# Causal attention whose softmax sums are gathered and folded by DMA, a streamed tile attention, and weight loads beside the norms

## The reference, cut to what matters

```python
# tile attention: a softmax of its own over each of 8 tiles of 128 keys
k_t = k.reshape(B, T, TILE, D)
v_t = v.reshape(B, T, TILE, D)
scores = jnp.einsum('bqd,btkd->btqk', q, k_t) * scale
w = jax.nn.softmax(scores, axis=-1)
out = jnp.einsum('btqk,btkd->bqd', w, v_t)
norm = w.sum(axis=-1).sum(axis=1)[..., None]
out = out / (norm + 1e-06)
return out @ Wo.T + bo

# causal attention, 16 heads of 8 features
scores = jnp.einsum('blhd,bmhd->bhlm', q, k) * scale
att = jax.nn.softmax(jnp.where(causal, scores, -jnp.inf), axis=-1)
out = jnp.einsum('bhlm,bmhd->blhd', att, v).reshape(B, L, D)
return out @ w_proj.T
```

## Time and profile before

| | |
|---|---|
| median of 3 runs | 5923.98 us (5920.12 to 5926.69) |
| the profiled execution | 5904.04 us, span 5902.2 us |
| granted TensorE clock, mean | 0.946 of full speed |
| busy: TensorE, VectorE, ScalarE, GpSimd | 84%, 68%, 54%, 30% of the span |
| tile attention | 45.9 to 323.4 us |
| the causal attentions | 460.2 to 1041.7 and 1616.8 to 2198.6 us |
| six local layers and the end | from some 2199 us on |

### The profile page before, as it was taken

How to read it: one execution, slowest core, us unless ns; L and a number is a source line. 1 busy time by engine, 2 the same in 40 slices (tenths; PEclk the granted TensorE clock), 3 DMA queues, 4 the chain that set the end, 5 groups by cost and what they waited for, 6 DMA issues and landing times. The chain is left out here.

```text
span 5902.2 us, 168251 instructions
## 1 busy us (share of the span) xinstructions
PE 4957.4 (84%) x74434; PEld 2867.4 (49%) x74640; DVE 3991.8 (68%) x4814; ACT 3191.4 (54%) x3632; POOL 1770.6 (30%) x1242
## 2 busy tenths in 40 slices
PE   6757887788688868998899889988998799979997
PEld 3423332333233325664466546654666366636663
DVE  5767775333477747885788568865887588748884
ACT  2324665222256546774577557754776367637773
POOL 0020000000200005551455235533554155505550
PEclk9988999899789999999999999999999899989998
DMA  0011000000101001111111111110111011101111
GB/s 25 0 53 35 25 24 13 22 0 0 62 18 29 24 30 38 38 38 34 34 37 37 41 27 38 38 45 23 36 37 53 16 38 38 35 30 38 38 38 41
DMA packets 90446, 187.28 MB, mean 32 GB/s; under 512 B 26112, under 2 KB 42368, under 8 KB 87552
## 3 DMA queue, kind: packets, MB, share of 16 engines
q1 hardware_dynamic: 89728, 176.58, 11.3%
HBM read 60.10 MB, written 14.68 MB: 13 GB/s over the span
## 5 line engine op out<-in xcount | busy, mean ns | idle before, releaser
L1413 POOL TENSOR_TENSOR part_of_local<-part_of_local,sine_of_local 128x512 f32<-128x512 f32 x768 | 961.2, 1273 | 1058.7 <-DVE sine_of_local L1350 1058.7
L820 ACT ACTIVATE prob_of_ca<-ps 128x1024 f32<-128x1024 f32 (+3 forms) x768 | 598.8, 814 | 374.9 <-PE ps L667 246.9
L1420 POOL TENSOR_TENSOR part_of_local<-part_of_local,inverse_of_local 128x1024 f32<-128x1024 f32 x384 | 722.5, 1903 | 139.6 <-DVE inverse_of_local L1382 139.6
L1387 DVE TENSOR_REDUCE total_of_local<-prob_of_local 128x16 f32<-128x1024 f32 x192 | 234.3, 1220 | 419.1 <-ACT prob_of_local L1326 419.1
L685 PE MATMUL ps<-keys_of_ca,queries_of_ca 64*128 64x512 bf16 (+3 forms) x1536 | 336.5, 346 | 195.2 <-DVE top_of_ca L858 73.2
L1347 DVE TENSOR_TENSOR part_of_local<-ps,rope 128x1024 f32<-128x1024 f32 x384 | 467.1, 1216 | 41.0 <-ACT square_of_local L1294 41.0
L1350 DVE TENSOR_TENSOR sine_of_local<-ps,rope 128x1024 f32<-128x1024 f32 x384 | 467.0, 1216 | 0.0
L1186 PE MATMUL ps<-qkv,shifted 128*128 128x512 f32 x768 | 392.0, 634 | 88.9 <-POOL values_of_local L1423 78.9
L1196 PE MATMUL ps<-qkv,shifted 128*128 128x512 f32 x768 | 381.0, 619 | 83.4 <-ACT heads_out_of_local L1322 69.3
L1272 PEld LDWEIGHTS ps<-prob_t_of_local,mixed_of_local 64*64 64x64 f32 x12288 | 335.6, 134 | 163.9 <-issue 154.1
L858 DVE TENSOR_REDUCE top_of_ca<-ps 128x2 f32<-128x1024 f32 (+1 forms) x320 | 357.1, 1116 | 70.1 <-PE ps L667 44.9
(11 more groups left out here) (206 smaller groups left out, 10122.5 us busy)
## 6 DMA issues: line engine op xcount, KB each, us to landing
mixed_of_local<-values_of_local SPq DMA_DIRECT2D x636, 128.0 KB
mixed_of_local<-values_of_local SPq DMA_DIRECT2D x264, 64.0 KB
queries_of_ca<-q_parts SPq DMA_DIRECT2D x384, 32.0 KB
keys_of_ca<-k_parts SPq DMA_DIRECT2D x384, 32.0 KB
qkv<-in_qkv SPq DMA_DIRECT2D x7, 1536.0 KB, 6.4
rope<-in_rope SPq DMA_DIRECT2D x7, 1024.0 KB, 9.0
q_parts<-parts_of_ci SPq DMA_DIRECT2D x16, 384.0 KB, 2.5
k_parts<-parts_of_ci SPq DMA_DIRECT2D x16, 384.0 KB, 2.5
```

The source lines that it names most:

```text
L820: nc.scalar.activation(prob[:, i % 2, 2 * two:2 * two + 2, j:], ps[:, 2 * two:2 * two + 2, j:], ACT.Exp, scale=scale).then_inc(raised, 1)
L1413: nc.gpsimd.tensor_tensor(out, out, sine[:, side, :, (1 - to) * half:(2 - to) * half], ALU.add).then_inc(rotated, 1)
L1420: nc.gpsimd.tensor_tensor(part[:, t % 2, side], part[:, t % 2, side], by, ALU.mult).then_inc(scaled, 1)
```

## The change

**Loads.** The first stage loads x in 8 chunks and only three constants; the other constants and the tile attention's weights are fetched by SyncE during `ln0`. The three later load stages of this part go; their DMAs are issued in `ln1`, `ln2` and `ln3`. In `ln1` and `ln2` ScalarE waits for them before it applies the norm's weights.

**Tile attention.** The loop over batches becomes one stage with a stream of 32 tiles. Projections and mixes of neighbouring batches are tasks, one after the score of most tiles, in PSUM bank 7. VectorE takes the maximum and scales it by −scale; ScalarE raises each of the 8 groups of 128 columns straight from PSUM with that as its bias, so the subtraction goes; VectorE makes sum and ratios; GpSimd multiplies the tile by them.

**Causal attention.** SyncE collects each group's sums by 8 DMAs: 8 rows a head into one full tile of 128 rows (`collected`), and the row of totals into DRAM. After the fourth group `fold` fetches the totals as 128x128, VectorE takes one reciprocal, SyncE writes it to DRAM and reads it back as a factor with 8 equal rows a head. GpSimd multiplies in two halves; a mix is one matmul. `collect` stands after `place` in SyncE's program, `fold` after the `collect` of a batch's last group, and both ahead of the next `load_stack`.

```diff
 def layernorm(..., fetches=(), late_weight=False):
...
                 nc.scalar.activation(rstd[:, :], rstd[:, :], ACT.Sqrt).then_inc(rooted, 1)
+                if late_weight:
+                    act.wait_ge(fetched, 16 * len(fetches))
...
 def tile_attention(nc, ps, k, w, xn, out):
-    with nc.Fori(0, B) as b, Stage(nc, "ta") as st:
+    with Stage(nc, "ta") as st:
...
+                for first in FIRST_TASKS:
+                    task(0, *first)
+                for s in range(NT + 3):
+                    if s < NT:
+                        score(s)
+                        if tile_task(s):
+                            task(*tile_task(s))
+                    if 0 <= s - 2 < NT:
+                        turn(s - 2)
+                    if s - 3 >= 0:
+                        gather(s - 3)
+                task(B - 1, "mix", 1)
...
+                def raise_tile(s):
+                    act.wait_ge(shifted, s + 1)
+                    if s >= 3:
+                        act.wait_ge(turned, s - 2)
+                    for j in range(TILES):
+                        last = nc.scalar.activation(prob[:, s % 3, j, :], score_banks(s)[:, j // 4, j % 4 * P:(j % 4 + 1) * P],
+                                                    ACT.Exp, bias=shift[:, s % 2, j:j + 1], scale=scale)
+                    last.then_inc(raised, 1)
...
+                for s in range(NT + 2):
+                    if s - 2 >= 0:
+                        copy_out(s - 2)
+                    if s < NT:
+                        raise_tile(s)
+                        if tile_task(s):
+                            task(*tile_task(s))
...
+                for s in range(NT + 4):
+                    if s < NT:
+                        top_of(s)
+                        if tile_task(s):
+                            task(*tile_task(s))
+                    if 0 <= s - 1 < NT:
+                        ratio_of(s - 1)
+                    if s >= 6 and (s - 6) % 4 == 0:
+                        even((s - 6) // 4)
...
+            @block.gpsimd
+            def _(pool):
+                for s in range(NT):
+                    pool.wait_ge(ratios, s + 1)
+                    nc.gpsimd.tensor_tensor(prob[:, s % 3], prob[:, s % 3], ratio[:, s % 2].unsqueeze(2)
+                                            .to_broadcast([P, TILES, P]), ALU.mult).then_inc(weighed, 1)
...
-FINISH = {(0, 4): ("totals", 0), (0, 5): ("invert", 0), (0, 6): ("invert", 1), (0, 7): ("split", 0), (0, 8): ("split", 1),
-          (1, 4): ("spread", 0), (1, 6): ("spread", 1), (1, 8): ("mix", 0),
-          (2, 4): ("spread", 2), (2, 6): ("spread", 3), (2, 8): ("mix", 1)}
+FINISH = {(0, 5): ("invert", 0), (1, 4): ("mix", 0), (1, 6): ("mix", 1)}
...
+                def collect(G):
+                    b, g = divmod(G, GROUPS)
+                    sp.wait_ge(acc_out, 2 * (G + 1))
+                    if g == 0 and b >= 2:
+                        sp.wait_ge(even, 2 * (b - 1))
+                    for h in range(HG):
+                        of = summed[h * QUAD:h * QUAD + HD + 1, G % 2].rearrange("p a n -> p (a n)")
+                        row = (g * HG + h) * HD
+                        sp.dma_start(collected[row:row + HD, b % 2, :], of[0:HD]).then_inc(collects[G % 2], 16)
+                        sp.dma_start(totals[g * HG + h:g * HG + h + 1, :], of[HD:HD + 1]).then_inc(collects[G % 2], 16)
+
+                def fold(b):
+                    for n in range(2):
+                        sp.wait_ge(collects[n], COLLECTS * 2 * (b + 1))
+                    sp.dma_start(folded[:, :], totals.rearrange("h (a n) -> (h a) n", n=P)).then_inc(totals_in, 16)
+                    sp.wait_ge(inverted, b + 1)
+                    if b:
+                        sp.wait_ge(factor_in, 16 * b)
+                    sp.dma_start(inverses.rearrange("h (a n) -> (h a) n", n=P), inverse[:, :]).then_inc(inverse_out, 16)
+                    sp.wait_ge(inverse_out, 16 * (b + 1))
+                    if b:
+                        sp.wait_ge(even, 2 * b)
+                    sp.dma_start(factor[:, :], inverses.unsqueeze(1).to_broadcast([HEADS, HD, L])).then_inc(factor_in, 16)
+
                 place(0)
-                for G in range(ALL - 1):
+                for G in range(ALL):
                     if G and G + 2 < ALL:
                         sp.wait_ge(scored, 2 * NU * G)
                         load_stack(sp, loaded[(G + 2) % RING_CA], stacks, zeros, q_parts, k_parts, G + 2)
-                    place(G + 1)
+                    if G + 1 < ALL:
+                        place(G + 1)
+                    collect(G)
+                    if G % GROUPS == GROUPS - 1:
+                        fold(G // GROUPS)
...
+                def evens(b):
+                    pool.wait_ge(factor_in, 16 * (b + 1))
+                    if b:
+                        pool.wait_ge(done, 2 * b)
+                    for half in range(2):
+                        nc.gpsimd.tensor_tensor(evened[:, chunk(half)], collected[:, b % 2, chunk(half)],
+                                                factor[:, chunk(half)], ALU.mult).then_inc(even, 1)
+
                 for G in range(ALL):
                     place_values(G)
+                    if G > GROUPS and G % GROUPS == 1:
+                        evens(G // GROUPS - 1)
+                evens(B - 1)
...
                 def mix(b, half):
                     take_lone()
-                    pe.wait_ge(even, 4 * b + 2 * half + 2)
-                    for g in range(GROUPS):
-                        last = nc.tensor.matmul(lone[:, :], proj[:, g, :], evened[:, g, :],
-                                                start=g == 0, stop=g == GROUPS - 1)
-                    last.then_inc(lone_ready, 1)
+                    pe.wait_ge(even, 2 * b + half + 1)
+                    nc.tensor.matmul(lone[:, :], proj[:, :], evened[:, chunk(half)], start=True, stop=True)\
+                        .then_inc(lone_ready, 1)
```

More of the change, by code:

```diff
@@ L212, in tile_attention, with task_bank, score_banks @@
+        FIRST = len(FIRST_TASKS)
+        number, made = {(0, *task): n for n, task in enumerate(FIRST_TASKS)}, FIRST
+        for s in range(NT + TILES):
+            if s < NT and tile_task(s):
+                number[tile_task(s)], made = made, made + 1
+        number[B - 1, "mix", 1] = made
+        def task_bank(n):
+            return ps[:, n if n < FIRST else 7, :]
+        def score_banks(s):
+            return ps[:, s % 2 * 2:s % 2 * 2 + 2, :]
         with nc.Block() as block:
@@ L224, in _, with task @@
[L224 to L228, removed]
+                def task(b, kind, half):
+                    n = number[b, kind, half]
+                    if n >= FIRST:
+                        pe.wait_ge(task_out, n)
+                    to, first = task_bank(n), b * L + half * CH
+                    if kind == "mix":
+                        pe.wait_ge(evened, 2 * b + half + 1)
+                        last = nc.tensor.matmul(to, w["ta_o"][:, :], outT[:, half, :], start=True, stop=True)
+                    elif kind == "v":
+                        for t in range(4):
+                            last = nc.tensor.matmul(to[:, t * P:(t + 1) * P], xn[:, first + t * P:first + (t + 1) * P],
+                                                    w["ta_v"][:, :], start=True, stop=True)
+                    else:
+                        last = nc.tensor.matmul(to, w["ta_" + kind][:, :], xn[:, first:first + CH], start=True, stop=True)
+                    last.then_inc(task_ready, 1)
@@ L261, in _ @@
-                score(0)
-                score(1)
-                for t in range(TILES):
-                    if t + 2 < TILES:
-                        score(t + 2)
-                    if t:
-                        gather(t - 1)
-                    turn(t)
-                    if t == 5:
-                        mix(0)
-                gather(TILES - 1)
-                mix(1)
+                        last = nc.tensor.matmul(ps[:, 6, s % 4 * P:(s % 4 + 1) * P], v[:, s // TILES % 2, j, :],
+                                                probT[:, s % 2, j, :], start=j == 0, stop=j == TILES - 1)
@@ L301, in _, with task @@
-                copy_out(TILES - 1)
-                finish(1)
-                act.wait_ge(written, 2)
+                def task(b, kind, half):
+                    n = number[b, kind, half]
+                    act.wait_ge(task_ready, n + 1)
+                    if kind == "mix":
+                        first = b * L + half * CH
+                        nc.scalar.activation(out[:, first:first + CH], task_bank(n), ACT.Identity,
+                                             bias=w["ta_bo"][:, :]).then_inc(task_out, 1)
+                    elif kind != "v":
+                        to = (qT, kT)[kind == "k"]
+                        nc.scalar.activation(to[:, b % 2, chunk(half)], task_bank(n), ACT.Identity,
```

(4 more changed lines are left out.)

327 lines of the change are left out of this document (114 added, 213 removed).

## The result

The median fell from 5925.33 us (5920.12 to 5931.23, 4 runs) to 5727.31 us (5725.95 to 5731.99, 4 runs): a ratio of 0.9667, 95% interval 0.9650 to 0.9684. The profiled execution took 5725.95, span 5724.2, clock 0.944: 178 us less than the span of before. The forecast was 5742 and the sum 182.

A forecast was written before the change was run, and what follows sets the result against it. It saw no full engine in the tile attention, TensorE and VectorE locked together in the causal attention, and loads standing alone. Gains 29 + 74 + 79 = 182 us took 5904.04 to 5722, plus 19.94 gave 5742, range 5685 to 5812.

The forecast's parts named there:

- last step: Whole kernel: the median lies 19.94 us above the profiled execution, so 5722 becomes 5742.
- loads: Load stages before the norms: loading beside the norms gives back 29 us, between 23 and 34.
- tile attention: Tile attention as one stream: 5.75 us a tile, 203.5 us against 277.5, a gain of 74.
- causal attention, both calls: Causal attention: cheaper batch finishes and a shorter end gain 39.5 us a call, 79 for both.
- the loop of 10.7 for two tiles: Tile attention: a closed loop through TensorE, VectorE and GpSimd takes 10.7 us for two tiles, 5.35 each.
- the plain groups: Causal attention groups without a fold: 0.25 us charged for each of ten stack loads a call.
- The mixes: Causal attention, group after a fold: two mixes, each one matmul and an eviction, cost 1.4 us each, 2.8.
- The term of 8.5: Causal attention, groups 4, 8 and 12: TensorE stands 8.5 us at unit 8 for stacks issued behind the fold.
- The end: Causal attention, last copy to the end of a call: 20.9 us against 29.14, 8.2 less.
- The fold costs nothing: Rival, causal attention: unit 8 isn't late, 2 × 25.5 us more gained, 5691; chance 0.12.
- the queue in every group: Rival, causal attention: SyncE's queue bounds every group, all 26 stack loads land 3 us later, 5815; chance 0.13.
- not streamed: Rival, tile attention: exps or GpSimd's product hold it at 6.6 us a tile, 27 us more, 5769; chance 0.10.

The follow-up runs named there:

- t_more: Changed kernel with an extra GpSimd product of half a tile, into a spare tile, in every tile of the tile attention: 5743.77 us.
- c_mix: Changed kernel with the two mixes moved from units 4 and 6 of the second group to unit 9 of the second and third: 5720.15 us.
- c_order: Changed kernel with SyncE issuing the next stacks before collect and fold, and the totals' reciprocal moved from unit 5 to unit 9: 5679.95 us.
- c_queue: Changed kernel with four more small DMAs in every collect, sending totals rows to a spare tensor: 5753.10 us.
- c_order_early: Changed kernel with SyncE issuing the next stacks before collect and fold, but the totals' inversion left at unit 5: 5734.18 us.

## Why the prediction was right

The mechanism held, and so did most sizes; the 15 us by which the forecast missed come from its last step. By its own steps:

| | predicted | measured |
|---|---|---|
| loads | 29 | 3.9 + 9.5 + 11.3 + 4.8 = 29.5 |
| tile attention | 74 | 277.5 − 198.1 = 79.4 |
| causal attention, both calls | 79 | 37.5 + 30.9 = 68.4 |
| sum | 182 | 177, span 178 |
| median less the profiled execution | 19.94 | 1.4 |

**Loads**: `late_weight` costs nothing, as said. A barrier without a load took 0.93 and 1.2 us to the next instruction, not 1.7.

**Tile attention**: the gain is 5.4 us more than predicted, and 5.57 a tile in place of 5.75 makes 5.6 of it. Both bounds that the prediction found so near are there: TensorE's own rate, and the loop of 10.7 for two tiles, which t_more measured as 10.6. The exps took 2.2 us for eight, predicted 2.3. By the terms of the Trainium skill (ScalarE: Activation LUTs, What ACT_TABLE_LOAD costs) I estimated 2.4 for them; the trace, with 2.16, is a little below.

**Causal attention**, first call. Fold's groups 8.2, 8.6 and 7.3 us over a plain one, predicted 8.5 each; groups with the mixes 4.1, predicted 2.8; the plain groups 0.3 in all, predicted 2.5; the end 22.7, predicted 20.9. That is 59.5 us where the forecast charged 57.3. The second call pays 5 us more: one fold's group is 10.1 over, and three plain ones wait 0.7 to 1.2 us for their stacks. The kernel before had paid 2.1 less for its finishes in that call than in the first, from which the prediction doubled.

**The mixes** were the term most undersized: 1.4 us each, one matmul and one eviction, measured as 2.1. c_mix shows that it is a matter of the place: at unit 9 one costs 0.9, about its matmul, so at units 4 and 6 the eviction and what waits for it are likely the rest.

**The term of 8.5** has the right size by a wrong make-up, and that is luck. It was to be one stall at unit 8 for the stacks; that is 4.6 us. Counted from the end of the copy (519.88), the stacks are issued from 10.9 on and the wait for them ends at 22.0, where I had 12.6 and 24.5: the totals' way to DRAM and back was shorter than charged, fetched in 1.8 us, written out in 1.5, where I had 2.3 and 2.5. And TensorE begins to wait at 17.4, not at 16.0, as it has been held up before. The Trainium skill (DMA: Bandwidth & Descriptors, Anatomy of one DMA) has a fixed 2.0 for each, fitted on DMAs issued from GpSimd; the trace's 64 KB, issued from SyncE, landed below that. In place of the difference stand TensorE's wait behind the reciprocal, 1.65, which I had called covered, and a rest of some 2 us, which fits the half clock after the stall and which I had not thought of. c_order took all three away together, 8.1 us of this group.

**The end** is 1.8 over: the 512 KB broadcast landed after 4.7 us, not 3.3, and the matmuls of both mixes ran at the low clock (2.05 us, where the same shape took 1.13 at 152.58).

**The rivals.** "The fold costs nothing" fell with the 4.62 us wait; "the queue in every group" with plain groups of 28.56, though by 1.1 us only, as c_queue shows; "not streamed" with 5.57.

**The last step was the largest miss.** Adding 19.94 us, because the profiled execution lay that far below its median, assumed that the gap belongs to the kernel. It did not: after's gap was 1.4. The profile of before was a run with the clock at 0.946, and seven later runs of the same kernel at 0.941 to 0.944 took 5914.6 to 5925.6; one at 0.946 again took 5909.1. So the forecast was 18.5 us too high by this and 4 too low by the sum: 15 too high.

## What to carry to other kernels

When work moves from busy engines to DMAs, the question is what stands behind those DMAs in the issuing queue: here 26 loads with a fixed due time stood behind a chain of four dependent transfers, and issuing them first, with the consumer of the chain moved four units later, was worth another 47 us. Of two loops that come out within 5% of each other, expect either to hold in part of the stage, and little from easing only one. A stall of TensorE can cost more than its length: behind 4.62 us here, and behind 7.89 in c_order_early, its clock stood at 0.50.

## What the runs showed of the hardware

- After 4.62 us without work TensorE was granted 0.50, then 0.62 of its clock over the next 6.7 us, with 1.00 in a plain part of the next group; eight matmuls took 1.93 instead of 1.06 us.
- In after's collect and fold, a DMA from SBUF to SBUF took 0.62 to 0.65 us of SyncE's queue to issue (up to 0.69 in c_order), one to or from DRAM 0.34 to 0.42, and the broadcast of 512 KB 0.60 to 0.64.
- Stretches that no edit touched differed by up to 16 us in 3180 between kernels with the same instructions there, TensorE's busy time with them (2804 to 2856 us) and VectorE's not (2281 and 2280). A difference of 10 us between two kernels is better read in its own stretch than in the total.
